# A 12-stage decoder on one core: the linear attention in a new order on every engine, and the cell of a recurrence written to PSUM and to SBUF

## The reference

```python
def step(carry, xg_t):
    h, c = carry
    g = xg_t + h @ W_hh.T
    i, f, gg, o = jnp.split(g, 4, axis=-1)
    c = jax.nn.sigmoid(f) * c + jax.nn.sigmoid(i) * jnp.tanh(gg)
    h = jax.nn.sigmoid(o) * jnp.tanh(c)
    return ((h, c), h)
```

```python
q, k, v = jnp.split(x @ Wqkv.T + bqkv, 3, axis=-1)      # each as (B, L, 16, 8)
q = (jax.nn.elu(q) + 1.0 + 1e-4) / sqrt(8)
k = jax.nn.elu(k) + 1.0 + 1e-4
kv_cumsum = jnp.cumsum(jnp.einsum('blhe,blhf->blhef', k, v), axis=1)
num = jnp.einsum('blhe,blhef->blhf', q, kv_cumsum)
den = jnp.einsum('blhe,blhe->blh', q, jnp.cumsum(k, axis=1))[..., None] + 1e-4
out = (num / den).reshape(B, L, D) @ Wout.T + bout
return (out - mean(out)) / sqrt(var(out) + 1e-5) * gamma + beta
```

## Time and profile before

| | |
|---|---|
| median of 3 runs | 2093.35 us |
| lowest, highest | 2092.13, 2100.03 us |
| profiled execution | 2096.0 us, of which span 2094.2 us |
| TensorE matmul, weight load busy | 1625.0 us (78%), 1037.0 us (50%) |
| VectorE, ScalarE, GpSimd busy | 1215.8 us (58%), 938.6 us (45%), 552.0 us (26%) |

### The profile page before, as it was taken

One profiled execution on the slowest core, in us unless ns is written; L12 is line 12 of the kernel. 1 busy time (PEld: TensorE's weight loads), 2 busy tenths in 40 slices (PEclk: granted clock), 3 DMA queues, 4 the chain that ended last, 5 costly groups with the idle time before them and its releaser, 6 DMA issues.

```text
span 2094.2 us, 43699 instructions
## 1 busy us (share of the span) xinstructions
PE 1625.0 (78%) x14747; PEld 1037.0 (50%) x14747; DVE 1215.8 (58%) x3764; ACT 938.6 (45%) x2731; POOL 552.0 (26%) x903
## 2 busy tenths in 40 slices
PE   4555389757778967897768833599799999996997
PEld 3333255434445545554445512366477777763443
DVE  2333556556664546405756778576566666654776
ACT  3222444346664534343434444333266566662433
POOL 2321422212114533201212223221144444341100
PEclk9999999869999988998989955699899999997999
DMA  5000000000000000000020000000000000000000
GB/s 206 2 1 1 0 2 0 0 1 0 0 0 2 2 0 1 1 0 2 0 103 1 0 1 0 1 1 0 0 2 1 0 0 0 0 1 1 0 0 20
DMA packets 2941, 18.46 MB, mean 9 GB/s; under 512 B 1049, under 2 KB 1177, under 8 KB 1561
## 3 DMA queue, kind: packets, MB, share of 16 engines
q1 hardware_dynamic: 2842, 17.17, 2.2%
HBM read 16.06 MB, written 1.05 MB: 8 GB/s over the span
## 4 chain that ended last, share of the span: by engine, by line
PE 58%; issue 16%; DVE 10%; ACT 7%; DVEq 4%; POOL 3%; POOLq 1%; DMA 0%; ACTq 0%; SPq 0%
PE ps L3061 5%; PE ps L936 4%; PE ps L950 3%; PE ps L2626 3%; PE ps L2636 3%; PE ps L2650 3%; PE ps L2605 3%; PE ps L2612 3%; PE ps L1005 2%; PE ps L2470 2%; PE ps L1525 2%; PE ps L358 2%; PE ps L915 2%; PE ps L1013 2%; PE ps L2597 1%
## 5 line engine op out<-in xcount | busy, mean ns | idle before, releaser
L376 POOL TENSOR_TENSOR arena<-arena,C 128x1 f32<-128x1 f32 (+1 forms) x176 | 99.5, 568 | 532.6 <-DVE arena L1131 303.3
L1095 DVE TENSOR_REDUCE arena<-ps 128x4 f32<-128x512 f32 x256 | 164.2, 686 | 89.0 <-PE ps L946 49.8
L2563 POOL TENSOR_TENSOR arena<-arena 128x512 f32<-128x512 f32 x128 | 132.7, 1042 | 233.7 <-DVE arena L2851 233.2
L471 POOL TENSOR_TENSOR arena<-arena,C 128x512 f32<-128x512 f32 x80 | 83.2, 1041 | 357.5 <-ACT arena L672 128.2
L1063 ACT ACTIVATE arena<-ps 128x512 f32<-128x512 f32 x256 | 132.2, 602 | 89.8 <-PE ps L962 89.8
L3061 PE MATMUL ps<-WA,arena 128*128 128x512 f32 x256 | 133.5, 603 | 0.4 <-ACT arena L3085 0.4
L1525 PE MATMUL ps<-hid,WA 128*20 128x16 f32 x1024 | 57.4, 197 | 90.1 <-DVE hid L1573 90.1
L2760 ACT ACTIVATE arena<-ps,arena 128x256 f32<-128x256 f32 x256 | 120.1, 478 | 11.8 <-issue 8.1
L2769 ACT COPY arena<-ps 128x512 f32<-128x512 f32 x128 | 69.1, 589 | 121.4 <-PE ps L2636 121.4
L2843 DVE TENSOR_REDUCE arena<-ps 128x2 f32<-128x512 f32 x128 | 82.5, 687 | 43.9 <-PE ps L2626 42.5
L1525 PEld LDWEIGHTS ps<-hid,WA 128*20 128x20 f32 x1024 | 43.8, 117 | 112.4 <-DVE hid L1573 112.0
(11 more groups left out here) (473 smaller groups left out, 4102.0 us busy)
## 6 DMA issues: line engine op xcount, KB each, us to landing
WA<-w_late SPq DMA_DIRECT2D x1, 4228.0 KB, 12.9
WA<-w_early SPq DMA_DIRECT2D x1, 1600.0 KB
R<-rows SPq DMA_DIRECT2D x1, 1282.0 KB, 7.1
WB<-w_rest SPq DMA_DIRECT2D x1, 1152.0 KB, 11.3
xT_all<-x_T SPq DMA_DIRECT2D x1, 1024.0 KB, 6.4
x_all<-x_tok SPq DMA_DIRECT2D x1, 1024.0 KB, 13.3
arena<-mask SPq DMA_DIRECT2D x1, 1024.0 KB
ctxT_all<-ctx_T SPq DMA_DIRECT2D x1, 1024.0 KB
```

The costliest lines, as they stand in the source:

```text
L1095: red = nc.vector.tensor_reduce(v_(z, ATT, "m", 4 * t, 4), heads(ps[z][t][:, :]), AXX, ALU.max)
L2563: nc.gpsimd.tensor_tensor(p, p, v_(z, LAT, "rec", 4 * u + 2 * x, 2).unsqueeze(2).broadcast_to([128, 2, 256]), ALU.mult).then_inc(l_sub, 1)
```

## The change

In the recurrence VectorE forms the cell twice: first into `cell`, 16 columns beside `tanh_c` in PSUM bank `ps[0][0]`, which releases the tangent, then into `gates[:, 3, :]` in SBUF, where the next step reads it, followed by a drain. The tangent reads `cell`.

In the linear attention TensorE's order in step k becomes scores(k), output(k-2), turned_x(k+3), turned_o(k-1), project(k+2), values(k), normed_T(k-1). The transposed x moves to the first 128 columns of `oT_bank`, the transposed result to the first half of `x_bank`, y to its second half. ScalarE copies x(k+3) between its first and second relu, and the transposed result last. VectorE adds x to the scaled y and masks bank 0 before it takes the moments of y, takes the division ahead of `yg`, and writes x back near the end of the step. The waits follow the banks. GpSimd's list stays.

```diff
--- before.py
+++ after.py
@@ -1444,6 +1444,7 @@
         tanh_c = ps[0][0][0:LSTM_H, 0:BATCH]
+        cell = ps[0][0][0:LSTM_H, BATCH:2 * BATCH]
         ms_all = arena[1][0:BATCH, 8832:9344].rearrange("p (t n) -> p t n", n=4)
...
@@ -1553,7 +1554,7 @@
...
                 act.wait_ge(cell_new, g + 1)
-                nc.scalar.activation(tanh_c[:, :], gates[:, 3, :], ACT.Tanh, scale=0.5).then_inc(cell_tanh, 1)
+                nc.scalar.activation(tanh_c[:, :], cell, ACT.Tanh, scale=0.5).then_inc(cell_tanh, 1)
                 if ABS_FROM <= g < ABS_FROM + 2 * len(TERN):
...
@@ -1567,8 +1568,11 @@
...
                 dve.drain()
+                nc.vector.scalar_tensor_tensor(cell, prod[:, 1, :], 0.5, prod[:, 0, :],
+                                               ALU.mult, ALU.add).then_inc(cell_new, 1)
                 nc.vector.scalar_tensor_tensor(gates[:, 3, :], prod[:, 1, :], 0.5, prod[:, 0, :],
-                                               ALU.mult, ALU.add).then_inc(cell_new, 1)
+                                               ALU.mult, ALU.add)
+                dve.drain()
                 dve.wait_ge(cell_tanh, g + 1)
...
@@ -2295,8 +2299,6 @@
...
                 pe.wait_ge(lin_oT_sb, n + 1)
-                if n > 0:
-                    pe.wait_ge(lin_yread, n)
                 for t in range(GROUPS):
...
@@ -2318,11 +2320,14 @@
...
                 pe.wait_ge(lin_div, n + 1)
-                nc.tensor.transpose(x_bank[:, 128:256], lin_(n, "O"), ident).then_inc(lin_on, 1)
+                if n > 0:
+                    pe.wait_ge(lin_yread, n)
+                nc.tensor.transpose(x_bank[:, 0:128], lin_(n, "O"), ident).then_inc(lin_on, 1)
 
...
                 pe.wait_ge(lin_v, n + 1)
-                done = 0
+                if seq(n + 3):
+                    pe.wait_ge(lin_xT_sb, n + 4)
                 for t in DVE_BANKS + ACT_BANKS:
...
@@ -2336,44 +2341,49 @@
...
                 pe.wait_ge(lin_on_sb, n + 1)
-                nc.tensor.matmul(o_bank[:, 0:128], lin_(n, "OnT"), W_of("lin", 384, 128), start=True, stop=False,
+                nc.tensor.matmul(x_bank[:, 128:256], lin_(n, "OnT"), W_of("lin", 384, 128), start=True, stop=False,
                                  skip_group_check=True)
-                add_bias(o_bank[:, 0:128], "lin", 384, 128).then_inc(f_y, 1)
+                add_bias(x_bank[:, 128:256], "lin", 384, 128).then_inc(f_y, 1)
 
...
                 pe.wait_ge(seq_done, ready(S_LIN, n))
-                nc.tensor.transpose(x_bank[:, 0:128], x_all[:, n, :], ident).then_inc(lin_xT, 1)
+                if n > 0:
+                    pe.wait_ge(lin_xT_sb, n)
+                if n > 3:
+                    pe.wait_ge(lin_oT_sb, n - 3)
+                nc.tensor.transpose(oT_bank[:, 0:128], x_all[:, n, :], ident).then_inc(lin_xT, 1)
 
...
                     scores(k)
+                if seq(k - 2):
+                    output(k - 2)
+                if seq(k + 3):
+                    turned_x(k + 3)
                 if seq(k - 1):
...
                     project(k + 2)
-                if seq(k - 1):
-                    normed_T(k - 1)
                 if seq(k):
...
                 if seq(k - 1):
-                    output(k - 1)
-                if seq(k + 3):
-                    turned_x(k + 3)
+                    normed_T(k - 1)
 
         def lin_act(act):
+            def evicted(k, m):
+                act.wait_ge(lin_sm, len(ACT_BANKS) * k + m + 1)
+                nc.scalar.activation(lin_PT(ACT_BANKS[m]), s_bank[ACT_BANKS[m]][:, :], ACT.Relu).then_inc(lin_relu, 1)
+
             for k in lin_steps():
-                n = k + 2
+                if seq(k):
+                    evicted(k, 0)
+                n = k + 3
                 if seq(n):
                     act.wait_ge(lin_xT, n + 1)
-                    nc.scalar.copy(lin_(n, "xT"), x_bank[:, 0:128]).then_inc(lin_xT_sb, 1)
+                    nc.scalar.copy(lin_(n, "xT"), oT_bank[:, 0:128]).then_inc(lin_xT_sb, 1)
                 if seq(k):
-                    for m, t in enumerate(ACT_BANKS):
-                        act.wait_ge(lin_sm, len(ACT_BANKS) * k + m + 1)
-                        nc.scalar.activation(lin_PT(t), s_bank[t][:, :], ACT.Relu).then_inc(lin_relu, 1)
-                n = k - 1
-                if seq(n):
-                    act.wait_ge(lin_on, n + 1)
-                    nc.scalar.copy(lin_(n, "OnT"), x_bank[:, 128:256]).then_inc(lin_on_sb, 1)
+                    for m in range(1, len(ACT_BANKS)):
+                        evicted(k, m)
                 n = k + 2
...
@@ -2384,6 +2394,10 @@
...
                                                                                         h=HEADS)).then_inc(lin_v, 1)
+                n = k - 1
+                if seq(n):
+                    act.wait_ge(lin_on, n + 1)
+                    nc.scalar.copy(lin_(n, "OnT"), x_bank[:, 0:128]).then_inc(lin_on_sb, 1)
 
...
@@ -2394,28 +2408,23 @@
...
                                                    ALU.add).then_inc(lin_f, 1)
-                y, r, done = k - 2, k - 3, k - 4
-                if seq(y):
-                    dve.wait_ge(f_y, y + 1)
-                    nc.vector.bn_stats(lin_(k, "stats", 0, 6), o_bank[:, 0:128])
-                    dve.drain()
-                    nc.vector.bn_aggr(lin_(k, "mv", 0, 2), lin_(k, "stats", 0, 6))
-                    dve.drain()
-                    nc.vector.scalar_tensor_tensor(lin_(y, "yg"), o_bank[:, 0:128], lin_(k, "mv", 0, 1), R[:, ROWS("lin_g")],
-                                                   ALU.subtract, ALU.mult).then_inc(lin_yread, 1)
+                y, r, done, o = k - 2, k - 3, k - 4, k - 1
+                y_bank = x_bank[:, 128:256]
+                if seq(r) or seq(done):
+                    dve.wait_ge(f_rstd, lin_count(k - 1))
+                if seq(r):
+                    dve.wait_ge(f_xb, r + 1)
+                    nc.vector.scalar_tensor_tensor(lin_(r, "r"), lin_(r, "yg"), lin_(k - 1, "rstd", 0, 1), lin_(r, "xb"),
+                                                   ALU.mult, ALU.add)
                 if seq(k):
...
                                                 ALU.mult).then_inc(lin_tri, 1)
-                if seq(r) or seq(done):
-                    dve.wait_ge(f_rstd, lin_count(k - 1))
-                if seq(r):
-                    dve.wait_ge(f_xb, r + 1)
-                    nc.vector.scalar_tensor_tensor(lin_(r, "r"), lin_(r, "yg"), lin_(k - 1, "rstd", 0, 1), lin_(r, "xb"),
-                                                   ALU.mult, ALU.add)
-                o = k - 1
+                if seq(y):
+                    dve.wait_ge(f_y, y + 1)
+                    nc.vector.bn_stats(lin_(k, "stats", 0, 6), y_bank)
                 if seq(o):
...
@@ -2425,9 +2434,8 @@
...
                     nc.vector.reciprocal(lin_(o, "rec"), lin_(o, "rec"))
-                if seq(done):
-                    nc.vector.tensor_scalar(x_all[:, done, :], lin_(done, "r"), lin_(k - 1, "mv", 2, 1),
-                                            lin_(k - 1, "rstd", 1, 1), ALU.subtract, ALU.mult).then_inc(seq_done, 1)
+                if seq(y):
+                    nc.vector.bn_aggr(lin_(k, "mv", 0, 2), lin_(k, "stats", 0, 6))
                 dve.drain()
...
@@ -2435,8 +2443,14 @@
...
                     nc.vector.bn_aggr(lin_(k, "mv", 2, 2), lin_(k, "stats", 6, 6))
-                    dve.drain()
+                if seq(y):
+                    nc.vector.scalar_tensor_tensor(lin_(y, "yg"), y_bank, lin_(k, "mv", 0, 1), R[:, ROWS("lin_g")],
+                                                   ALU.subtract, ALU.mult).then_inc(lin_yread, 1)
+                if seq(done):
+                    nc.vector.tensor_scalar(x_all[:, done, :], lin_(done, "r"), lin_(k - 1, "mv", 2, 1),
+                                            lin_(k - 1, "rstd", 1, 1), ALU.subtract, ALU.mult).then_inc(seq_done, 1)
                 a, b = lin_moments(k)
+                dve.drain()
                 if a < b:
...
```

## The result

The changed kernel takes 2084.65 us at the median of 6 runs (2083.46 to 2085.79), the kernel before 2095.5 us (2092.13 to 2100.57, 6 runs); the ratio is 0.9941, with a 95% interval of 0.9927 to 0.9954. By the ratio that is 12.4 us less, by the two medians 10.9, against 13.0 forecast (2080.4 us; range 2077 to 2087). The profiled execution took 2084.36 us, its span 2082.5 instead of 2094.2, which is 11.7 less.

A forecast was written before the change was run, and what follows sets the result against it. Bounds: a serial one-engine-at-a-time chain in the recurrence, VectorE's chain of waits in the linear attention, TensorE's 5.07 us next. Gains 4.0 + 9.0 = 13.0 us took 2093.35 to 2080.4 us; range 2077 to 2087.

The forecast's parts named there:

- The step of 32 ns for the tangent's source: Recurrence: the tangent reading the cell from PSUM instead of SBUF saves 32 ns per step, 4.0 us over the steps.
- the bounds: Recurrence: tangent's PSUM read and VectorE's small PSUM write bounded together by 0 and 40 ns of gain, 0 to 5.1 us.
- The cover: Recurrence: second product and drain ready 0.15 us after the cell, hidden state starting at 0.22, so hidden with 0.07 to spare.
- rival 1: Recurrence: second product starts only at the cell's end, is not hidden, no gain there; total 2084.4 us; chance 0.17.
- Rival 4: Recurrence: PSUM write's signal reaches ScalarE only after the second product, tangent starts 0.16 us later; 2101.0 us; chance 0.05.
- the 5.07 us that I took for TensorE's own work: Linear attention: TensorE's work per step, summed from start-to-start costs, was to set the step at 5.07 us instead of 5.70.
- the 0.15 that I had given that change: Linear attention: TensorE's change from full to 32-row tiles costs some 0.15 us, moving to between projection and values.
- rival 2: Linear attention: step held at about 5.35 us, signs N waiting for yg or r for xb; 2083.4 us; chance 0.15.
- 0.25 to spare: Linear attention: N's wait for the division and yg is over at 4.56 us, N wants it at 4.81.
- The path to xb over the exp and the cut: Linear attention: exp at 3.93 us releases GpSimd's queue; xb ends at 6.71, 1.64 into the next step, before VectorE's r.
- The start and the end: Linear attention: gains outside the repeating steps, 0.2 us at the stage's start and 0.8 us at its end.
- Rival 3: Linear attention: some wait puts the step back at 5.70 us, only the recurrence gains; 2089.4 us; chance 0.08.

## Why the prediction was right, and where it was not

**The recurrence.** Forecast 4.0 us, measured 2.8. The step of 32 ns for the tangent's source held: 177 to 146 ns is 31. The term that was mis-sized is the product into PSUM, which I had left at no cost inside the bounds: 172 instead of 163 ns, all of it ahead of the tangent. 31 - 9 = 22 ns, times 128 = 2.8 us. The cover was read rightly, with its overlap of 0.08, its drain of 0.07 and 0.07 to spare (79.97 + 0.16 + 0.07 = 80.20 against 80.27), so rival 1 fell. Rival 4 fell too: the tangent starts 0.04 after the cell as before.

**The linear attention.** Forecast 9.0 us, measured 9.6, with steps of 5.08 against 5.07. The number was right and its account was wrong: two errors met, and that is luck.

The failed step is the 5.07 us that I took for TensorE's own work. It held a wait. Before the change T waits for yg to be read out of its bank (`lin_yread` in `turned_o`, which the diff removes). In the earlier trace rows yg ends at 674.80 + 0.35 = 675.15 and T starts at 675.27, 0.12 later, as in the other steps in which it waits. I booked the 0.77 us from M to T as M's length. The first T of the stage has no such wait, and the kernel before shows what TensorE needs there (M, T, P):

```profile
652.80 0.33 PEld L2292 LDWEIGHTS ps<-ident_b,causal_b 128*128 128x128 bf16 x3 [0.76 <-issue]
...
653.25 0.58 PEld L2301 LDWEIGHTS ps<-C,arena 128*128 128x128 f32 x4
...
653.79 0.30 PEld L2312 LDWEIGHTS ps<-arena,WA 128*128 128x128 f32 x2
```

T follows M by 0.45 us, and P follows M by 0.99; in the step of the earlier trace rows P's first weights are loaded at 675.66, 1.16 after M. The last T behind a mask (731.93, M at 731.49), whose yg had ended at 731.50, is 0.44 behind as well. So the wait put 1.16 - 0.99 = 0.17 us into the 5.07, and TensorE's own work in the old order was 4.90. In the new order it is 4.87: M again 0.45, O 0.44 instead of 0.33, X 0.06 instead of 0.26, T 0.44 instead of 0.54, and P to V 1.14 instead of 0.98, about the 0.15 that I had given that change.

What held the step was rival 2, by both of its signs, at 5.08 instead of the 5.35 that I gave it: r waits for xb, and N waits for yg, where I had 0.25 to spare. The path to xb over the exp and the cut is the one of the prediction. xb came earlier than I had it (1.39 into the step that starts with S at 664.64, rather than 1.64), but r took 1.04 us instead of 0.35. I had costed r by its length before, when the wide feature was nearly over whenever r started; the new order puts r right behind the start of it, 0.15 us later. The rows of before have the 1.04 us wide feature and an r with two SBUF inputs, but none in which r starts with more than the last 0.2 us of it to run. T's reading was at 3.26 into the step, not 2.98, for that reason; the rest was shorter, and N came at 4.78, near the forecast 4.81. TensorE's work was 0.20 shorter than forecast, and the loop added 0.21.

**The start and the end.** By the parts of the forecast: from the scores of step 2 to those of step 15 it took 65.8 us (654.67 to 720.44) where 65.5 was forecast, a gain of 7.8 for 8.0; the end gained 16.77 - 15.63 = 1.1 for 0.8, and the start 0.7 for 0.2. The start can't be tested: from the first copied x to the first N, kernels with the same order of TensorE take 14.8 to 17.3 us, and the time goes with the granted clock of that stretch, 14.8 us in all five runs at 0.88, 15.3 at 0.78, 16.9 at 0.70 and 17.2 or 17.3 at 0.67. The changed kernel's profile has 0.70, the one before 0.68.

**Rival 3** (a wait puts back 5.70) fell. **The rest of the kernel** was taken as unchanged; it lost 1.4 us ahead of the linear attention and won 0.6 behind it in this pair of profiles. In the kernels of this study with untouched code there, the stretch from the last hidden state to the first copied x took from 427.7 to 433.5 us. Behind the linear attention it is 1346.2 to 1350.1. Each scatter is larger than the recurrence's whole gain. It goes with TensorE's speed: ahead of the linear attention its matmuls are busy for 310.8 us in the profile with 427.7 and for 319.7 in the one with 433.5, the same 3082 of them, while VectorE is busy for 259.1 and 259.5. What lowers the granted clock in one execution and not in the next, no run shows.

**By part of the sum:** the measured 11.7 us of the span are 2.8 + 9.6 - 1.4 + 0.6, rounded.

## What to carry to other kernels

A length read from one start to the next holds every wait in between, also one that its row calls "issue": before it goes into a sum as an engine's own work, look at what each piece waits for in the code, and for a step in which that wait is absent or long over. And when the longest wait is gone, the next may be a loop over several engines and more than one step. For every VectorE instruction with two SBUF inputs ask what GpSimd does at that moment in the new order; here a wait added on GpSimd made the stage 2.8 us faster. Here a small tile between VectorE and ScalarE on a serial chain was worth 22 ns a step when it lay in PSUM instead of SBUF, and the copy of it for other readers was free because it ended before the chain came back.

## What was not expected of the hardware

- A VectorE product of 20x16 takes 172 ns into PSUM and 163 into SBUF; ScalarE's tangent of the same tile 146 ns from PSUM and 176 from SBUF.
- r stood for GpSimd's whole wide feature: 1.04 us for 0.35 of work, 1.20 where both started together, 0.35 in all 16 cases when kept apart.
- In the recurrence TensorE's granted clock was 1.00 before and 0.51 after, from 20 to 200 us, that is 2.4 and 1.2 GHz, with nothing changed in its instructions; the matmuls with the hidden state (L1525, then L1526) took 194 ns at the median in both. The level follows neither version of the recurrence nor its time: with the old one it was 1.00 (196.4 us) and, in the run of the linear attention alone, 0.50 (196.3 us); with the new one 1.00 in the run of the recurrence alone (193.9 us) and 0.51 after (193.6 us). The two rows, first before, then after:

```profile
20.00:200.00 180.00, 98.64 (x1410) 67.11 (x1407) 61.64 (x366) 54.88 (x366) 49.69 (x101) 1.00 0.07 24
```

```profile
20.00:200.00 180.00, 98.82 (x1424) 67.38 (x1424) 72.99 (x490) 51.62 (x369) 49.69 (x101) 0.51 0.07 25
```
